# Other places for transposes, value, first gather and output projection; sigmoid per unit; one broadcast comparison with the other half

## The reference

```python
# layer 0
xn = layernorm(x)
s = retention(xn)      # ((xn Wq)(xn Wk)^T * decay mask) (xn Wv), gamma 0.96875
g = silu(ffn(xn))      # z = silu(xn w1) * (xn w2); h1 = gelu(z H1); h2 = gelu(h1 H2); h2 w3
x = x + s * g
# layer 1
xn = layernorm(x)
x_ssm, gate = split(xn @ W_in + b_in)
x_conv = silu(conv4(x_ssm));  B, C = split(x_conv @ W_x + b_x)
h = A * h + x_conv[:, :, None] * B[:, None, :]      # scan over the tokens, 16 states per feature
y = (einsum(C, h) + D * x_conv) * silu(gate);  s = y @ W_out + b_out
score = xn @ w_router;  chosen = top 512 of the 1024 tokens
update = sigmoid(score) * (gelu(xn @ W1 + b1) @ W2 + b2)   # for chosen tokens only
x = x + s * silu(xn + update)
```

## Time and profile before

| | us |
|---|---|
| median of 3 runs | 567.41 (567.29 to 569.21) |
| profiled execution | 567.98 |
| its span | 566.2 |
| periods 4 and 5 | 60.90 and 61.30 |
| the last 72 us (rest of period 7, and period 8) | VectorE busy 58.5 |

### The profile page before, as it was taken

How to read it: one execution, slowest core, us unless ns; L and a number is a source line. 1 busy time by engine, 2 the same in 40 slices (tenths; PEclk the granted TensorE clock), 3 DMA queues, 4 the chain that set the end, 5 groups by cost and what they waited for, 6 DMA issues and landing times.

```text
span 566.2 us, 6086 instructions
## 1 busy us (share of the span) xinstructions
PE 477.3 (84%) x1905; PEld 279.3 (49%) x1919; DVE 409.3 (72%) x635; ACT 296.7 (52%) x476; POOL 395.5 (70%) x380
## 2 busy tenths in 40 slices
PE   0795879898999899899989899989989998884865
PEld 0574545545564556455654566455645465331321
DVE  2281134868688877967897878787897769669995
ACT  2664636664576556454757465654745553433120
POOL 1671643977598759976798669885996689646563
PEclk9997979999999999999999999999999999988786
DMA  8400000000000001000100000000100000000000
GB/s 313 159 20 4 1 19 1 1 1 19 1 1 0 1 19 38 1 2 19 39 0 2 19 19 19 0 2 0 39 0 1 1 20 1 0 1 19 1 19 20
DMA packets 5939, 11.83 MB, mean 21 GB/s; under 512 B 913, under 2 KB 1937, under 8 KB 5649
## 3 DMA queue, kind: packets, MB, share of 16 engines
q1 hardware_dynamic: 4752, 9.47, 4.6%
q10 hardware_dynamic: 1152, 1.93, 1.0%
HBM read 9.30 MB, written 2.10 MB: 20 GB/s over the span
## 4 chain that ended last, share of the span: by engine, by line
PE 55%; DVE 18%; ACT 11%; issue 7%; POOL 7%; DMA 1%; SPq 0%; DVEq 0%; ACTq 0%; POOLq 0%
PE bank0a L906 20%; PE bank1a L986 6%; PE ybank L1055 5%; DVE hs L1345 4%; DVE beats L1302 4%; DVE xbank L1322 3%; PE xbank L1040 3%; PE bank0a L1019 2%; PE bank1d L1028 2%; PE bank1a L971 2%; POOL hs L522 2%; POOL hidAl L483 2%; PE bank1a L996 2%; ACT plain L616 2%; DMA Bt<-w_in 1%
## 5 line engine op out<-in xcount | busy, mean ns | idle before, releaser
L522 POOL TENSOR_TENSOR hs<-hs,Ct 128x512 f32<-128x512 f32 x127 | 167.8, 1323 | 26.7 <-DVE hs L1345 21.3
L1322 DVE TENSOR_TENSOR xbank<-xbank,Bt 128x512 f32<-128x512 f32 x128 | 88.0, 687 | 29.7 <-PE xbank L1040 29.5
L1040 PE MATMUL xbank<-xpair,spr 128*128 128x512 f32 x128 | 78.1, 610 | 25.3 <-DVE hs L1345 25.1
L483 POOL TENSOR_TENSOR hidAl<-plain,hidAh 128x512 fp32r<-128x512 f32 x48 | 63.6, 1326 | 41.0 <-ACT hidAh L617 31.0
L483 POOL TENSOR_TENSOR hidBl<-plain,hidBh 128x512 fp32r<-128x512 f32 x48 | 66.9, 1396 | 32.7 <-ACT hidBh L617 18.6
L616 ACT ACTIVATE plain<-bank0a,col 128x512 f32<-128x512 f32 x64 | 44.0, 688 | 84.8 <-PE bank0a L906 80.9
L1345 DVE TENSOR_TENSOR_SCAN hs<-decay,carry,xbank 128x512 f32<-128x512 f32 x63 | 80.6, 1279 | 7.3
L1345 DVE TENSOR_TENSOR_SCAN hs<-decay,xbank 128x512 f32<-128x512 f32 x64 | 78.0, 1219 | 4.9
L1040 PEld LDWEIGHTS xbank<-xpair,spr 128*128 128x128 f32 x128 | 24.7, 193 | 69.5 <-DVE hs L1345 43.2
L906 PE MATMUL bank0a<-hidBh,hTh 128*128 128x512 f32 x128 | 55.9, 436 | 2.1 <-ACT hidAh L617 2.1
L906 PE MATMUL bank0a<-hidAh,hTh 128*128 128x512 f32 x128 | 54.7, 428 | 2.2 <-ACT hidBh L617 2.2
(11 more groups left out here) (187 smaller groups left out, 964.7 us busy)
## 6 DMA issues: line engine op xcount, KB each, us to landing
xt<-x_tok SPq DMA_DIRECT2D x8, 256.0 KB, 2.6
xr<-x_feat SPq DMA_DIRECT2D x8, 256.0 KB, 7.5
out<-xr SPq DMA_DIRECT2D x7, 256.0 KB, 2.0
fh<-h_w SPq DMA_DIRECT2D x1, 1024.0 KB, 10.3
hs<-h_w SPq DMA_DIRECT2D x1, 1024.0 KB, 12.4
lw<-l_w ACTq DMA_DIRECT2D x1, 640.0 KB, 6.8
g<-spread ACTq DMA_DIRECT2D x1, 512.0 KB, 6.0
Bt<-w_in SPq DMA_DIRECT2D x1, 512.0 KB, 8.2
```

Of the source, the lines that this page charges most:

```text
L483: pool.tensor_tensor(low[:, m, :], plain[:, k % NPLAIN, :], high[:, m, :].bitcast(F32), ALU.subtract).then_inc(hidden_low, 1)
L522: pool.tensor_tensor(h, h, Ct[:, hs_(u)], ALU.mult).then_inc(p_ready, 1)
L1040: pe.matmul(xbank[i % 2][:], spr[:, at, :], xpair[:, half, hs_(u)], start=True, stop=True).then_inc(xs_full, 1)
L1322: dve.tensor_tensor(xbank[i % 2][:], xbank[i % 2][:], Bt[:, hs_(u)], ALU.mult).then_inc(xb_ready, 1)
```

## The change

The functions do the same work, in these other places:

- TensorE: `to_tokens` before `z2` in slot 1; quarter 1 of the gather after `mod_down` and quarter 2 after `norm_to_features`; `project_out` in slot 5 before gate; `retention_in` of unit w in slot 9 after `retention_out`, and in `L0_ACT` ahead of all h2 products; quarter 0 of the gather from slot 12 to 14, behind the second `mod_up`; `value` from behind `ffn_out` in slot 15 to slot 14 behind the first `mod_up`.
- ScalarE: `retention_in` follows `take_u` in slot 9; the sigmoid is made per unit in slot 12.
- GpSimd: `weigh_update` in slot 6 in place of 10.
- VectorE: the four comparisons with the other half are one `tensor_tensor` over 2048 columns, both inputs broadcast.

```diff
-        L0_ACT += [("z1", _v, 2), ("z1", _v, 3)] + [("h1", _v, _m) for _m in range(KT)] + [("u", _v), ("h2", _v, 0)]
+        L0_ACT += [("z1", _v, 2), ("z1", _v, 3)] + [("h1", _v, _m) for _m in range(KT)] + [("u", _v)]
     if _w is not None:
         L0_ACT.append(("xnT", _w))
     if _v is not None:
-        L0_ACT += [("h2", _v, _m) for _m in range(1, KT)]
+        L0_ACT += [("h2", _v, _m) for _m in range(KT)]
...
# GpSimd
-                pool.wait_ge(sig_ready, t // 2 + 1)
+                pool.wait_ge(sig_ready, t + 1)
...
-                if t is not None and s == (1 if t == UNITS - 1 else 10):
+                if t is not None and s == (1 if t == UNITS - 1 else 6):
                     weigh_update(t)
...
# ScalarE
+            def sigmoid(t):
+
+                act.wait_ge(l1_act_done, done(L1_ACT, ("score", t)))
+                if t >= 2:
+                    act.wait_ge(o_ready, t - 1)
+                act.activation(g1[:, hs_(t)], srow[:, hs_(t)], ACT.Tanh, scale=0.5).then_inc(tanh_ready, 1)
+                act.wait_ge(tanh_ready, t + 1)
+                act.activation(g1[:, hs_(t)], g1[:, hs_(t)], ACT.Copy, bias=0.5, scale=0.5).then_inc(sig_ready, 1)
...
# TensorE, slot(p, s)
-                    if s == 1 and t is not None:
-                        gather_y(t, 1)
+                    if s == 1 and n is not None:
+                        to_tokens(n)
                     if v is not None and s < KT:
                         z2(v, s)
...
-                    if n is not None:
-                        if s == 1:
-                            to_tokens(n)
-                        elif s == 3:
-                            norm_to_features(n)
-                    if s == 4 and t is not None:
-                        gather_y(t, 2)
+                    if n is not None and s == 3:
+                        norm_to_features(n)
+                    if s in (1, 4) and t is not None:
+                        gather_y(t, 1 if s == 1 else 2)
+                    if s == 5 and e is not None and e != UNITS - 2:
+                        project_out(e)
...
+                    if w is not None and s == 9:
+                        retention_in(w)
                     if v is not None and 10 <= s < 10 + KT:
                         hidden("h2", v, s - 10)
-                    if w is not None and s == 10:
-                        retention_in(w)
-                    if s == 12 and n is not None:
-                        gather_y(n, 0)
...
                     if n is not None and s >= 14:
                         mod_up(n, 2 * (s - 14))
+                    if v is not None and s == 14:
+                        value(v)
+                    if n is not None and s >= 14:
                         mod_up(n, 2 * (s - 14) + 1)
+                    if n is not None and s == 14:
+                        gather_y(n, 0)
                     if v is not None and s == 15:
                         ffn_out(v)
-                        value(v)
...
# VectorE
-                if not 0 <= j < CPH:
-                    dve.tensor_scalar(bt, row, s_i, None, ALU.is_le if j < 0 else ALU.is_lt).then_inc(beats_ready, 1)
-                    return
...
+            def compare_other(u):
+
+                other = u // 2 * 2 + 1 - u % 2
+                dve.wait_ge(l1_act_done, done(L1_ACT, ("score_col", other)))
+                if u > 0:
+                    full1(("rank", u - 1))
+                s_i = scol[:, u // 2 % 2, cs_(other)].rearrange("p (c o) -> p c o", o=1)
+                row = srow[:, hs_(u)].rearrange("p (o i) -> p o i", o=1)
+                dve.tensor_tensor(beats[:, CPH:], row.broadcast_to([P, CPH, HALF]), s_i.broadcast_to([P, CPH, HALF]),
+                                  ALU.is_le if u % 2 else ALU.is_lt).then_inc(beats_ready, CPH)
```

More of the change, by code:

```diff
@@ L680, in score_columns @@
                                ACT.Copy).then_inc(l1_act_done, 1)
-            def sigmoid_half(b):
-                act.wait_ge(l1_act_done, done(L1_ACT, ("score", 2 * b + 1)))
-                if b > 0:
-                    act.wait_ge(o_ready, 2 * b)
-                act.activation(g1[:], srow[:], ACT.Tanh, scale=0.5).then_inc(tanh_ready, 1)
-                act.wait_ge(tanh_ready, b + 1)
-                act.activation(g1[:], g1[:], ACT.Copy, bias=0.5, scale=0.5).then_inc(sig_ready, 1)
+            def sigmoid(t):
[5 more added lines that the diff above has]
+                act.activation(g1[:, hs_(t)], g1[:, hs_(t)], ACT.Copy, bias=0.5, scale=0.5).then_inc(sig_ready, 1)
             def take_gate(t):
@@ L775, in slot @@
                         score_columns(n)
-                        if n % 2 == 1:
-                            sigmoid_half(n // 2)
+                    elif s == 12:
+                        sigmoid(n)
                 if w is not None and s == 9:
@@ L782, in slot @@
                         take_u(v)
-                    if 10 <= s < 10 + KT:
-                        hidden("h2", v, s - 10)
-                if w is not None:
-                    if s == 10:
-                        retention_in(w)
+                if w is not None and s == 9:
+                    retention_in(w)
+                if v is not None and 10 <= s < 10 + KT:
+                    hidden("h2", v, s - 10)
                 if n is not None:
@@ L1129, in slot @@
                             score_column(n)
-                    if s == 5 and e is not None and e != UNITS - 2:
-                        project_out(e)
                     if s == 8 and t is not None:
@@ L1400, in slot @@
                 if t is not None:
-                    for pos in range(CH):
-                        if compare_slots(t)[pos] == s:
-                            compare(t, pos)
+                    if compare_slots(t)[CPH] == s:
+                        compare_other(t)
                     if s == weights_slot(t):
```

## The result

| kernel | median, us | lowest to highest | profiled execution, span | ratio to before, 95% interval |
|---|---|---|---|---|
| before | 568.3 | 567.3 to 569.8 | 566.2 | 1 |
| after | 551.6 | 550.8 to 553.5 | 551.7 | 0.971 (0.967 to 0.975) |

The account below looks back on a forecast made before the run. Periods 0 to 6 were taken as TensorE-bound with 4.5 to 5.1 us of gaps, the tail as VectorE's. Gains of 12 (periods 1 to 6), 1 (period 0) and 3 (tail), together 16.0, gave 552 us; range 544 to 565.

Parts of the forecast that it names:

- The comparison's duration: VectorE's single 128x2048 tensor_tensor: 2.28 us plus a remaining GpSimd instruction of 0 to 1.28, taken as 2.9 us.
- rival 4: VectorE's comparison pays the disturbed price throughout, 7.1 us, so the kernel gets slower, 578 us; chance 0.05.
- the sign of a wrong step: Comparison's mean over 8 VectorE instructions: near 2.9 us expected; at 2.3 or 7.1 its step is wrong.
- 1.0 of slot 11's wait goes, 0.3 per period for GpSimd's backlog: TensorE's odd-period spread behind the comparisons waits 1.0 us less; GpSimd falling behind in slots 11 to 14 costs 0.3.
- Rival 3: GpSimd, late from comparison and weigh_update, delays the last h1 low part; first h2 product waits 2 us more, 564; chance 0.08.
- Value and the first gather: Moved into slot 14, they fill TensorE's waits for ScalarE and at slot 12: 1.4 us even, 0.9 odd removed.
- Given back 0.5 or 0.6 in slot 1: With value gone from behind ffn_out, TensorE reaches slot 1's spread early: new wait 0.5 us, 0.6 in odd periods.
- of its 1.3 us in the odd period I count 1.0 as gone: TensorE's spread behind the four comparisons waits 1.3 us in odd periods; the shorter VectorE block removes 1.0.
- The transposes: Earlier to_tokens removes slot 3's 0.9 us spread wait; earlier retention_in the second h2 product's 0.7, or 0.4 + 0.2 odd.
- The u read: First h2 product needs u read, ending 0.6 us after the u product; mostly covered, new wait 0.1 us.
- project_out: Moved before gate, fills a 0.6 us TensorE hole, but C's 0.5 us wait for B's reader returns; net 0.1.
- weigh_update: At slot 6 on GpSimd it delays slot 7's state product: gather 3 waits 0.7 us odd, 0.2 even.

Follow-up runs that it names:

- the pair: The kernel before with only the broadcast comparison and value with the first gather moved into slot 14: 554.6 us, ratio 0.979.
- the split comparison: The kernel before with the broadcast comparison as two instructions of 128x1024 in place of the four tensor_scalar: 574.9 us, ratio 1.012.

## Why the prediction was right, and where it was not

The direction and the size came out, in the main by the gaps that it named, but the price list behind it was partly wrong, and that 552.0 met 551.6 is luck (see the result).

- **The comparison's duration**: 2.9 forecast, 2.30 measured at the median, 2.53 in the mean; 7.1 (rival 4) is out. The added turn of GpSimd (0.6 us on average) shows in periods 3 and 5 only (3.20 and 3.19); the other six take 2.27 to 2.43, which the prediction itself had named as the sign of a wrong step.
- **What the comparison does**: the step "1.0 of slot 11's wait goes, 0.3 per period for GpSimd's backlog" mis-sized the backlog. GpSimd loses 2.0 us per unit instead of the 0.8 of before (period 4). In the kernel before this costs 1.7 us in period 4 and 3.3, 2.3 and 2.3 in periods 2, 3 and 5 (these with a lower clock, last section), and the edit alone is a loss of 7.3. Rival 3 had named the mechanism, but only at the h2 product. There it costs 0.2 us in the changed kernel's even periods, 1.15 with weigh_update at slot 8 and 1.86 where retention_in stands behind that product; with the gather at slot 12 it decides at the first gather, which the same change takes out of its way. Nowhere did the prediction see that the gather's move is what makes the comparison pay. Its sum held only because both came together.
- **Value and the first gather**: removed 1.4 and 0.9 as forecast. "Given back 0.5 or 0.6 in slot 1" didn't happen: no wait of slot 1 is in the rows of periods 4 and 5. What was given back instead is slot 14's spread, 0.5 even and 1.5 odd. The step "of its 1.3 us in the odd period I count 1.0 as gone" failed there: VectorE's block of slots 10 to 14 is one chain, and only the place where TensorE meets it had moved. Nor are the odd periods alike, as the prediction has them: in before the wait is 0.6 us in period 1, 1.3 in periods 3 and 5.
- **The transposes**: 0.9 at slot 3 gone in the even periods and in period 1; in periods 3 and 5 only 0.3 of it went (undone: +7.8 us against 6.6 worked out, and the periods and the rest add up to 6.3). retention_in: 4.1 us against about 3.5; right in size, but by another wait and partly by the clock: undone, even periods lose 1.5 us, with a wait of 1.86 at GpSimd's low part, and period 5 nothing (60.1 us). The u read costs 0.35, not 0.1.
- **project_out**: C waits 0.3 in periods 4 and 5 (0.6 in period 3), forecast 0.5. The sigmoid was put at nothing; no run has it by itself.
- **weigh_update**: gather 3 waits 0.4 odd and nothing even, forecast 0.7 and 0.2. Not seen: at slot 6 it stands ahead of norm_l0's scale as well, the activation at 393.66 waits for that, and retention_in's products wait 0.45 for xn in periods 2 to 5; with weigh_update at slot 8 or 10 the wait is gone.
- **The tail**: the comparison's 1.4 and 0.4 (2.27 us twice) and the transposes' 1.2 came. The 0.7 and 1.0 us of new waits behind the gather of slot 14 took more than half of it back; the run with the last gather at 13 gives 1.8 of it back.
- **Period 0**: 1 forecast, 3.4 measured. The prediction put periods 0 to 6 at 4.5 or 5.1 us of gaps each; period 0 has 9.2 (57.44 us with 48.20 busy). It counted no first gather there, which waited 1.4 us for GpSimd, and mod_up 1.0 for ScalarE. Value and the gather alone give 4.2 us in period 0.

Leaving out the comparison, the gather's move, to_tokens or retention_in costs 7.2, 7.7, 7.8 and 4.1 us: 26.8 in all, for a change that is worth 16.7. Such losses don't add up to a gain: several of these edits act on the same meeting of TensorE with VectorE or GpSimd, as the pair shows, and three of the four kernels also have periods at a lower clock, which the changed kernel has not.

What stays open is why the pair alone gains 13.8 us and the other edits only 3.0 more, though undoing one of them from the whole costs 7.8. By the profiles the changed kernel is 1.1 us shorter than the pair in each even period, 1.0 in period 1, 1.2 in period 6 and 0.6 in the rest, but 1.1 and 0.8 us longer in periods 3 and 5, where slot 14's spread waits 1.5 us instead of 0.8, and 0.9 longer in period 0. Why period 0 is longer, and why 0.5 us stay at slot 3 in periods 3 and 5, is open too.

## What to carry to other kernels

Here TensorE had caught up with VectorE's block, and a removed wait came back at their next meeting. In such a case price an edit at the last place where the two meet in that block, not at the first. Before a VectorE instruction is made longer or given two SBUF inputs, add up what it takes from GpSimd and follow GpSimd's queue to the first product that needs it. And undo each part of a change by itself and also do it by itself: here the one says 7 us gained and the other 7 us lost, of the same edit. Look at the granted clock of each period before you call such a difference a wait.

## What the runs showed of the hardware

A period with a long wait of TensorE can lose more than the wait, through its clock. In the comparison-alone kernel TensorE waits 2.50 us before the product at 235.30; the granted clock then is at the lower level for a stretch (0.50 is 1.2 GHz, 1.00 is 2.4):

```profile
234.00:236.00 2.00, 0.70 (x1) 0.30 (x2) 1.90 (x3) 0.17 (x1) 2.00 (x2) 0.89 0.00 0
236.00:238.00 2.00, 2.00 (x10) 0.20 (x8) 0.97 (x1) 0.00 (x0) 1.92 (x3) 0.50 0.00 0
238.00:240.00 2.00, 2.00 (x13) 0.94 (x6) 0.55 (x1) 0.00 (x0) 1.92 (x4) 0.75 0.00 0
```

Its price shows in the kernel with value and gather alone, whose periods 3 and 5 have the same two longest waits, 1.34 and 1.76 us:

```profile
242.58:304.89 62.31, 56.28 (x237) 33.60 (x238) 50.60 (x78) 36.51 (x60) 48.23 (x46) 1.00 0.04 13
364.43:428.43 64.00, 57.97 (x237) 34.18 (x238) 50.71 (x78) 36.55 (x60) 48.28 (x46) 0.97 0.03 9
```

One drop is 1.7 us, all of it TensorE's busy time. Periods 1 to 6 of the 14 profiles are 84. In 65 of them no wait of TensorE is over 1.55 us, and all are at 1.00. In the other 19 the longest wait is 1.76 to 2.50 us, and 11 of them are at 0.97. So luck has a part in such kernels: the comparison alone has three such periods (2, 3 and 5), the whole without the comparison two (3 and 5), retention_in undone two (3 and 4), the split comparison two (2 and 4), value with the gather alone one, the gather back at slot 12 one, the changed kernel none. At 1.7 us each, an estimate from the pair of rows above, that is some 5, 3, 3, 3, 2 and 2 us of what these profiled executions took; of the runs without a profile it can't be said. That the waits cause the drops is not shown, and what else decides whether the clock falls can't be said from these runs.

The second point is that splitting the instruction did not spare GpSimd anything beside the comparison: 1.95 against 2.0 us lost, while VectorE's part grew from 2.27 to 3.43.
